# A new order of the steps on every engine of a hand-scheduled two-layer mixture-of-experts kernel

## What is computed

```python
x = x + 0.5 * _L0_ffn_ref(_layernorm(x), ...)     # 8 experts, top 1, 128->512->128, gelu
x = x + _L0_attn_ref(_layernorm(x), ...)          # conv, cumulative-sum attention, gelu block
x = x + 0.5 * _L0_ffn_ref(_layernorm(x), ...)
x = x + 0.5 * _L1_ffn_ref(_layernorm(x), ...)     # 16 experts, capacity 320, relu, softmax gate
x = x + _L1_attn_ref(_layernorm(x), ...)          # linear recurrence along the sequence
x = x + 0.5 * _L1_ffn_ref(_layernorm(x), ...)
```

## Time and profile before

| | us |
|---|---|
| median of 3 runs | 703.21 |
| lowest and highest of them | 701.41, 703.81 |
| profiled execution, its own time | 701.15 |
| its span, first to last instruction | 699.5 |

### The profile page before, as it was taken

The page is one execution under the profiler, slowest core; times in us unless marked ns, Lnnn a source line. Parts: engine busy times, 40 slices in busy tenths (PEclk is TensorE's granted clock), DMA queues, the critical chain, the costliest instruction groups (busy, mean ns, idle before and its releaser), DMA issues.

```text
span 699.5 us, 13116 instructions
## 1 busy us (share of the span) xinstructions
PE 624.4 (89%) x3647; PEld 480.7 (69%) x3647; DVE 449.4 (64%) x1882; ACT 328.0 (47%) x1038; POOL 367.8 (53%) x377
## 2 busy tenths in 40 slices
PE   4656899999889999998899998999998897899996
PEld 3556889886767666988899633676655784466674
DVE  6833556886999898764445615577737982557774
ACT  2223448667766553355445104555525740455451
POOL 0467646254312162777446774377660466237676
PEclk9659899999999999999999899999999986999999
DMA  9764675315103114465874415333629311915420
GB/s 293 284 207 120 195 218 148 122 52 207 51 1 84 26 55 107 111 199 188 231 205 161 154 61 183 110 115 104 184 47 234 126 57 53 243 49 176 112 84 15
DMA packets 85879, 93.95 MB, mean 134 GB/s; under 512 B 12152, under 2 KB 65307, under 8 KB 85552
## 3 DMA queue, kind: packets, MB, share of 16 engines
q1 hardware_dynamic: 73648, 74.23, 36.7%
q0 software_dynamic: 10880, 15.07, 6.4%
q10 hardware_dynamic: 1280, 3.81, 1.7%
HBM read 64.18 MB, written 33.76 MB: 140 GB/s over the span
## 4 chain that ended last, share of the span: by engine, by line
PE 47%; POOL 18%; DVE 12%; issue 11%; DMA 8%; ACT 2%; SPq 1%; ACTq 0%; DVEq 0%; POOLq 0%
POOL xs L1606 11%; PE ps L901 10%; PE ps L894 9%; POOL y L1610 5%; PE ps L829 4%; PE ps L821 4%; PE ps L843 3%; PE ps L876 3%; PE ps L736 3%; DMA y<-yt,xi 3%; PE ps L778 2%; DMA X<-y 2%; PE ps L884 2%; PE ps L869 2%; PE ps L908 2%
## 5 line engine op out<-in xcount | busy, mean ns | idle before, releaser
L1606 POOL DMA_INDIRECT xs<-X,IDX x128 | 125.7, 982 | 119.4 <-issue 71.5
L1499 ACT ACTIVATE ht<-ps,CL 128x128 f32<-128x128 f32 x336 | 92.5, 382 | 91.9 <-PE ps L821 86.2
L1610 POOL DMA_INDIRECT y<-yt,xi x84 | 83.0, 988 | 66.1 <-DVE yt L1242 51.8
L821 PE MATMUL ps<-xt,w1s 128*128 128x128 f32 x672 | 88.9, 285 | 4.4 <-DVE xt L1236 3.5
L829 PE MATMUL ps<-W,ht 128*128 (+1 forms) x672 | 87.4, 282 | 2.6 <-ACT ht L1499 1.7
L821 PEld LDWEIGHTS ps<-xt,w1s 128*128 128x128 f32 x672 | 83.5, 200 | 6.7 <-DVE xt L1236 4.0
L829 PEld LDWEIGHTS ps<-W,ht 128*128 128x128 f32 x672 | 81.7, 195 | 7.1 <-issue 6.7
L921 PE MATMUL ps<-MT,KC 128*128 128x512 f32 x136 | 65.4, 633 | 1.4 <-DVE SE L1334 0.5
L1597 POOL TENSOR_TENSOR sma<-sma,MH 128x4 f32<-128x4 f32 (+1 forms) x24 | 30.9, 1293 | 45.3 <-DVE sma L951 35.7
L1556 ACT ACTIVATE hb<-ps 128x320 f32<-128x320 f32 x64 | 27.0, 430 | 50.5 <-PE ps L894 50.4
L1549 ACT ACTIVATE w1s<-x,SE 128x128 f32<-128x128 f32 (+1 forms) x66 | 27.5, 483 | 49.5 <-DVE SE L1345 49.3
(11 more groups left out here) (214 smaller groups left out, 1292.2 us busy)
## 6 DMA issues: line engine op xcount, KB each, us to landing
w1s<-in_w SPq DMA_DIRECT2D x84, 256.0 KB, 3.0
W<-in_w1x SPq DMA_DIRECT2D x17, 512.0 KB, 5.2
wx<-in_w1x SPq DMA_DIRECT2D x15, 512.0 KB, 4.0
X<-y SPq DMA_DIRECT2D x24, 256.0 KB, 4.6
xs<-ZX SPq DMA_DIRECT2D x32, 185.0 KB, 5.1
xi<-xs SPq DMA_DIRECT2D x84, 66.0 KB
x<-xs SPq DMA_DIRECT2D x22, 148.0 KB, 2.3
X<-in_x SPq DMA_DIRECT2D x8, 264.0 KB, 7.2
```

The lines of the kernel that those rows point to most:

```text
L821: r = e.matmul(ps[TILE_BANKS[i % n]][:, c * P:(c + 1) * P], W1[i % NW1][:, c * P:(c + 1) * P], XTT[i % NX][:, :], start=True, stop=True)
L1499: r = e.activation(HT[i % NHT][:, c, :], ps[TILE_BANKS[i % len(TILE_BANKS)]][:, c * P:(c + 1) * P], ACT.Gelu, bias=CL[:, bass.ds(r0 * 4 + ...
L1606: return e.indirect_dma_start(dst, bass.IndirectOffsetOnAxis(ap=IDX[:, n:n + 1], axis=0), X[:, n, 0:w], None, bounds_check=hi, oob_is_err= ...
L1610: return e.indirect_dma_start(dst, bass.IndirectOffsetOnAxis(ap=ix, axis=0), src, None, bounds_check=hi_home, oob_is_err=False, engine_sem ...
```

## The change

The five strings of `TABLE` are replaced by others. Each holds the same steps, every step once, in another order. No other line differs: no instruction, buffer, semaphore or wait of a step is changed. Since PE's list also gives the ring of PSUM banks, a dense step may use another bank. Of the diff two lines, the first of the ACT string:

```diff
-cenc.0 tri.0 pstd.0 pstd.1 pcopy.0 pcopy.1 pcopy.2 pcopy.3 pcopy.4 pcopy.5 pstd.2 hb2.0 decay.0 bulk.0 bulk.1 tgelu.0 tgelu.1 tgelu.2 tgelu.3 tgelu.4
+pstd.0 tri.0 cenc.0 pstd.1 pcopy.0 pcopy.1 pcopy.2 pcopy.3 bulk.0 pcopy.4 pcopy.5 pstd.2 decay.0 bulk.1 hb2.0 tgelu.0 tgelu.1 tgelu.2 tgelu.3 tgelu.4
```

More of the change, by code:

```diff
@@ L179 @@
[L179 to L182, removed]
@@ L200 @@
-aconv.2 adown.1 aturn1.3 aconv.3 aturn1.4 pturn.7 aturn2.2 aq.2 ak.2 av.2 aconv.4 aturn1.5 aturn3.2 aturn2.3 aconv.5 aq.3 aturn4.2 ak.3 aup.8 av.3
-aturn1.6 aconv.6 aturn3.3 aup.9 aturn2.4 aturn2.5 aup.10 aq.4 aup.11 ak.4 av.4 aturn4.3 adown.2 aq.5 aturn1.7 ak.5 pturn.8 aconv.7 av.5 aup.12 aup.13
-aturn3.4 aturn3.5 aup.14 aup.15 aturn2.6 pscore.8 aq.6 pscore.9 pscore.10 ak.6 aturn4.4 av.6 adown.3 aturn3.6 aup.16 rrank.2 aturn4.5 aup.17 aup.18
-aturn2.7 aup.19 aup.20 adown.4 aup.21 pturn.9 aup.22 pturn.10 aq.7 aturn4.6 ak.7 aup.23 aup.24 av.7 pscore.11 pscore.12 aturn3.7 aup.25 aup.26 aup.27
@@ new lines @@
+aconv.2 aturn1.3 adown.1 aconv.3 aturn2.2 pturn.7 aq.2 aturn1.4 ak.2 aturn1.5 av.2 aconv.4 aturn3.2 aturn2.3 aconv.5 aq.3 aturn4.2 ak.3 av.3 aturn1.6
+aup.8 aconv.6 aturn3.3 aturn2.4 aup.9 aup.10 aup.11 aq.4 ak.4 aturn2.5 adown.2 aturn4.3 av.4 aq.5 aup.12 aturn3.4 ak.5 aturn1.7 av.5 pturn.8 aconv.7
+aturn2.6 aturn3.5 aup.13 pscore.8 pscore.9 pscore.10 aup.14 aup.15 aq.6 ak.6 adown.3 av.6 aturn4.4 aturn4.5 aturn3.6 aup.16 aup.17 aup.18 rrank.2
+aup.19 aup.20 adown.4 aturn2.7 aq.7 ak.7 pturn.9 pturn.10 pscore.11 pscore.12 av.7 aturn4.6 aup.21 aup.22 aup.23 aup.24 aturn3.7 aup.25 aup.26 aup.27
@@ new lines @@
+pstat.0 pstat.1 pstat.2 pinv.0 plog.0 oh.0 pstat.3 pstat.4 pstat.5 pinv.1 ra.0 pstat.6 pstat.7 rb.0 rsel.0 rte.0 pnm.0 rslot.0 pinv.2 plog.1 plog.2
+oh.1 oh.2 pnm.1 rnext.0 ra.1 rb.1 rslot.1 rsel.1 tn.0 tn.1 tn.2 tn.3 tx.0 pnm.2 tx.1 tx.2 txb.0 txb.1 tx.3 txb.2 tn.4 ty.0 tn.5 tn.6 ty.1 txb.3 txb.4
+tx.4 txb.5 tn.7 tx.5 tx.6 ty.2 txb.6 tx.7 wc.0 ty.3 ty.4 ty.5 rte.1 ty.6 tn.8 tn.9 tx.8 tn.10 txb.7 tx.9 txb.8 tx.10 ty.7 txb.9 tn.11 tn.12 tn.13
+tx.11 txb.10 txb.11 ty.8 tn.14 ty.9 tx.12 tx.13 tn.15 tx.14 txb.12 txb.13 ty.10 tn.16 ty.11 tn.17 tx.15 tx.16 tn.18 tn.19 ty.12 ty.13 txb.14 tx.17
@@ L298 @@
+enorm.28 erela.54 erela.55 egexp.27 egexp.28 enorm.29 erela.56 erela.57 erela.58 erela.59 egexp.29 enorm.30 enorm.31 egexp.30 erela.60 erela.61
+egexp.31 erela.62 erela.63""",
     "pool": """
@@ L304 @@
[L304 to L306 removed]
+home.7 home.8 home.9 home.10 home.11 home.12 home.13 home.14 home.15 home.16 home.17 home.18 apow1.0 apow1.1 home.19 home.20 home.21 home.22 home.23
```

233 lines of the change are left out of this document (115 added, 118 removed).

## The result

The changed kernel takes 704.02 us (median of 20 runs), the kernel before on the same chip 700.89 us (20 runs). The ratio is 1.0043, with a 95% interval from 1.0027 to 1.0058: slower by 3.0 us (1.9 to 4.1). The forecast was 705.2 on a median of 703.21, that is +2.0 us. Most of what follows adds up to that 1.4.

The account below looks back on a forecast made before the run. TensorE bounds the kernel, with a chain through all engines at the start and row scatters. Terms 8 - 1.5 - 1.5 + 0 + 0.5 - 3 - 0.5 = +2.0 us on the 703.21 median give 705.2 us, range 698.0 to 711.5.

Parts of the forecast that it names:

- the start: Up to tile 8: a chain through all engines sets the time; loses 8 us, all of it passing through.
- the second pass: Second pass's tiles: TensorE's 2.06 us wait for tile 63 goes, other waits come; -1.5 us (-3 to +2).
- the second expert stage: `edown.16` loses its 2.48 us wait and slow clock, a table load stands ahead of `erela.32`; -3 us (-4.5 to 0).
- the case of new waits: Rival: attention and tile terms at +2 each, since DVE has no air; sum +9, 712.2 us; slower overall 0.44.
- the first rival: TensorE fast at the start, `pscore.7` ending before 30.8: sum -2.2, 701.0 us; faster 0.30, mostly by this rival.
- (1): Start, ScalarE: `cenc.0` behind `pstd.0`'s wait and table load, first scores at 12 instead of 8.35, `plog.0` 3.65 us later.
- (2): Start, VectorE: two statistics and a reciprocal, 2.6 us, ahead of `ra.0`; `pturn.1` begins at 21.4 instead of 15.14.
- (3): Start, TensorE: same work to `pscore.7`, ending 33.2 at the same clock mixture or 36.1 all slow; loss 6.3 or 9.2.
- The mixture: Start: TensorE's work up to `pscore.7` done partly at full clock as before, ending at 33.2; loss 6.3 us.
- the other rule: Start: transposes do not count as work that brings the full clock; `pscore.7` all slow, +9.2, taken only as upper bound.
- The attention stretch: Middle: new order covers 2.9 us of four TensorE waits, others may come as DVE is nearly full; -1.5 (-5 to +2).
- The first expert stage: First expert stage, where PE hardly waited: -0.5 us.
- The recurrence: First index table 4.3 us later through DVE's added work, POOL's pauses of 4.1 us go; +0.5 us (-2 to +4).

Follow-up runs that it names:

- run 11: Kernel before with one VectorE edit: two statistics and a reciprocal ahead of the addition that releases TensorE's second transposes; 769.14 us, ratio 1.0056.
- runs 10: Kernel before with one ScalarE edit: first standard deviation ahead of the two copies that TensorE's first scores need; 766.98 us, ratio 1.0018.
- run 7: Changed kernel plus five groups of four unused 128-column products in TensorE's two idle stretches at the start; 775.14 us, ratio to before 1.0051.
- Run 1: Changed kernel with every engine's steps up to tile 8's transpose in the order of before; 690.45 us, ratio 0.9875 to before.
- Run 4: Changed kernel with six of 35 warm-up products ahead of the first expert stage narrowed from 512 to 64 columns; 697.06 us, ratio 0.9964 to before.
- run 3: Changed kernel with two of SyncE's four zero-fills put back ahead of the loads waiting for the first expert stage; 701.41 us, ratio 1.0021 to before.

## Why the prediction was right, and where it wasn't

The direction and the size are those of the forecast, +2.0 forecast and +3.0 measured. The terms are not: three of them were missed by 3 to 7 us, and cancelled. That the sum came out is luck; what the forecast had right is the start, the second pass and the second expert stage. (Its range also ended at 711.5 where its own sum for the case of new waits says 712.2, and the 697 of the first rival would be 696 by the upper ends given.)

**The start, +8 forecast, +9.2 measured at `send.8`, +9.3 at tile 8.** All three parts are there. (1) The first scores come at 11.93, forecast 12.0, and `plog.0` 3.61 us late, against 3.65. (2) `pturn.1` begins at 21.18, forecast 21.4; run 11 has VectorE's part by itself, 2.42 for 2.6. (3) The last scores end at 36.08; "all slow" was worked out as 36.1. This bound was right and the value between the bounds was 1.2 us short. The mixture would have been right for each edit alone (runs 10 and 11 kept the fast stretch), and the two together lost it. The reason given for the choice, that slow rows follow idle time, was read too widely: the 0.50 from 21.90 on in the earlier trace rows followed unbroken work, as the forecast's own rival says. The first rival, TensorE fast, would have needed an end before 30.8; even with filler products (run 7) the end came only to 32.38.

Of the two rules cited for the start, the price of a table switch did not show in full: the load at 10.03 took 1.28 us again and the next operation followed at 11.32, and the load that the change saves gave nothing back at `send.8`. (By the price in the Trainium skill, ScalarE: Activation LUTs, What ACT_TABLE_LOAD costs, the start would have come to +5.3, as an estimate.) A start of +9.2 is what the other rule gives (the Trainium skill, TensorE: Matmul & The Clock Gate, Part 4: PE-mode transpose), yet in runs 10 and 11 the fast stretch came again at the end of 20 transposes, where the changed kernel, with scores between its transposes, had none. The number fitted and the traces speak against the reason.

**The attention stretch, -1.5 forecast, -8.5 measured.** This is the step that failed most. Of the four waits named three are gone and the one ahead of `aq.2` shrank from 0.87 to 0.68 us, 2.8 us together, a third of it. From the start of tile 8 to the end of the last attention step, the same work, TensorE is idle for 10.5 us in the kernel before (202.22 busy of 212.75) and for 5.7 in the changed one (198.61 of 204.27): 4.9 us of idle time gone, not 2.9 minus something for new waits. Run 1, where the start is the same, has 5.4 (199.67 of 205.08). The other 3.6 us are busy time. The kernel before had two dips of the granted clock between 156 and 276, run 1 one, and the changed kernel none:

```profile
230.00:240.00 10.00, 9.79 (x56) 7.31 (x56) 8.32 (x27) 4.95 (x12) 2.02 (x2) 0.83 0.01 2
260.00:270.00 10.00, 8.84 (x46) 5.90 (x46) 8.62 (x31) 3.42 (x7) 6.26 (x6) 0.83 0.14 40
```

Each 0.83 over 10 us is 3.4 us at half the clock, by estimate about 1.7 us lost for each dip if all of it is work that bounds. No run separates the dips from the rest. That term was not in the sum at all, though 0.97 for the window stood in the earlier trace rows. And "DVE has no air" was wrong: it got 106.06 us of work into the same 120. The rival of new waits in the middle fell with it.

**The second pass, -1.5 forecast.** -1.1 between the traces, and 3.8 in run 1. Tile 63 is turned at 334.22 with no idle time in front.

**The sends from `send.64`, 0 forecast.** They start 3.19 us earlier while the tiles end 0.34 earlier, as the first table (`q3.0`) now comes 2.44 us ahead; POOL alone then sets `eload.0`. This and the attention term would have made the change faster than before.

**The first expert stage, -0.5 forecast, +4.9 measured from `eload.0` to `rstat.0`.** The cause wasn't in the forecast: 35 products of a fixed length between the scores and the stage. The changed order ends the scores later (401.12 instead of 397.77), with the granted clock at 0.50 from 398 to 402, so that the row starts and ends later, whatever the sends have won. Run 4 shows it as a bound: narrowing six of them brought the stage forward by 2.0 us in the trace and the whole kernel by 5.5 by the ratios. The forecast looked for what is late next among the waits, and this was none: PE was busy.

**The recurrence, +0.5 forecast, +3.1 measured, within the term's -2 to +4.** The first table is 3.3 us later against the recurrence's first step (forecast 4.3), as VectorE's steps ahead of it say, and that lateness stays: the last ranks end 3.05 us later against the same point, and the row of warm-up products, and with it `eturn.16`, follows them. The 4.1 us that the forecast set against it, the pauses of POOL, are gone in the trace but paid nothing at `eturn.16`: in the kernel before, too, the products held TensorE for 1.6 us after the rows of expert 16 were there. They are gone partly because the two fills moved behind the loads held `send.96` for 4.3 us more, which gave the tables time; in run 3, with the fills moved back, the 32 sends take 42.0 us instead of 39.7 (43.7 in the kernel before). The forecast left out both SyncE's queue and the row; that the term came out within its bounds is not for its reasons.

**The second expert stage, -3 forecast, -3.2 measured.** `edown.16` lost its wait of 2.48 us and takes 2.42 instead of 4.08, and three up projections more stand ahead of it. `erela.32`, behind the table load, ended at 611.44, but TensorE came to `edown.16` only at 613.79, so the load cost what stood in front of `eup.68`, 0.48 us.

The two signs named as fatal did not come: tile 8 started at 81.44, not before 76, and TensorE's idle time from 156 to 385 was 11.9 us.
